# Causal mask by relu, exp and a multiply on GpSimd in place of triangle matmuls on TensorE

## The reference, cut to what matters

```
xn = layernorm(x)                                   # x: 4 x 1024 x 256
q, k, v = xn @ Wq.T + bq, xn @ Wk.T + bk, xn @ Wv.T + bv   # 16 heads of 16
q, k = rope(q), rope(k)
att = where(tril, q @ k.T / 4, -inf)                # causal: key index <= query index
y = softmax(att) @ v                                # merged heads
attn = y @ Wo.T + bo
# feed-forward: 1024 hidden units in 16 blocks of 64; each token keeps its 4 best blocks
mask = top4(softmax(xn @ router_w.T + router_b))
ffn = relu(where(mask, xn @ w1.T + b1, 0)) @ w2.T + b2
out = x + attn + ffn
```

## Time and profile before

| | us |
|---|---|
| median of 3 runs (854.21 to 854.64) | 854.6 |
| profiled execution, time | 853.66 |
| profiled execution, span | 851.9 |
| PE busy | 816.7 |
| DVE busy | 591.8 |
| ACT busy | 426.9 |
| POOL busy | 281.6 |

### The profile page before, as it was taken

The page is one execution under the profiler, slowest core; times in us unless marked ns, Lnnn a source line. Parts: engine busy times, 40 slices in busy tenths (PEclk is TensorE's granted clock), DMA queues, the critical chain, the costliest instruction groups (busy, mean ns, idle before and its releaser), DMA issues.

```text
span 851.9 us, 14875 instructions
## 1 busy us (share of the span) xinstructions
PE 816.7 (96%) x5278; PEld 494.4 (58%) x5278; DVE 591.8 (69%) x1800; ACT 426.9 (50%) x1018; POOL 281.6 (33%) x298
## 2 busy tenths in 40 slices
PE   5784999999999999999999999999999999999998
PEld 4463745554546555664766565565666656465664
DVE  7993887868799856667687766767566876668312
ACT  2410355556565554645564464555456554456462
POOL 3155451926344029406515007706250103000000
PEclk9987999999999999999999999999999999999999
DMA  7445331523251445131251414324242224200021
GB/s 261 165 147 153 106 89 52 163 88 100 77 181 34 113 137 164 57 109 36 77 172 42 105 40 135 110 76 101 75 115 100 49 72 142 54 3 26 3 69 50
DMA packets 52375, 81.91 MB, mean 96 GB/s; under 512 B 5836, under 2 KB 21132, under 8 KB 52300
## 3 DMA queue, kind: packets, MB, share of 16 engines
q1 hardware_dynamic: 52300, 80.95, 31.8%
HBM read 43.06 MB, written 37.88 MB: 95 GB/s over the span
## 4 chain that ended last, share of the span: by engine, by line
PE 85%; DVE 4%; ACT 3%; issue 3%; SPq 2%; DMA 2%; POOL 1%; ACTq 0%; DVEq 0%; POOLq 0%
PE o_bank L1118 15%; PE banks L1043 14%; PE banks L1102 14%; PE banks L1031 12%; PE banks L1018 12%; PE banks L992 5%; PE banks L1105 3%; PE banks L1070 3%; ACT probs L919 3%; PE banks L1001 3%; PE banks L1022 2%; DVE o_norm L1410 1%; DMA bv_sb<-in_bv 1%; DMA term_scratch<-pieces 1%; SPq L604 1%
## 5 line engine op out<-in xcount | busy, mean ns | idle before, releaser
L919 ACT ACTIVATE probs<-banks 128x512 f32<-128x512 f32 (+3 forms) x768 | 328.3, 497 | 247.9 <-PE banks L1105 174.3
L1102 PE MATMUL banks<-q_st,k_st 99*128 99x512 bf16 (+3 forms) x768 | 237.1, 328 | 3.4 <-ACT probs L919 0.8
L1043 PE MATMUL banks<-k_st,q_st 96*128 96x512 bf16 (+3 forms) x768 | 229.0, 328 | 1.5 <-issue 0.8
L1314 DVE CUSTOM_DVE_ANT_0 banks<-banks,tri,part_max 128x512 f32<-128x512 f32 (+3 forms) x256 | 129.7, 554 | 72.6 <-PE banks L1043 41.8
L1311 DVE TENSOR_REDUCE part_max<-banks 128x1 f32<-128x512 f32 x256 | 159.6, 680 | 16.3 <-PE banks L1043 15.7
L1314 DVE CUSTOM_DVE_ANT_0 banks<-banks,tri 128x512 f32<-128x512 f32 (+3 forms) x256 | 120.2, 516 | 30.6 <-PE banks L1043 29.1
L1018 PE MATMUL banks<-xnT,w_sb 128*128 128x256 f32 x512 | 137.6, 392 | 0.7 <-ACT probs L919 0.4
L797 POOL TENSOR_SCALAR max_neg<-row_max 128x16 f32<-128x16 f32 x32 | 8.1, 253 | 384.2 <-DVE row_max L1314 384.2
L1118 PE MATMUL o_bank<-probs,v_sb 128*17 128x512 f32 (+3 forms) x1536 | 133.2, 487 | 0.0
L1031 PE MATMUL banks<-w_sb,hT 128*128 128x256 f32 x512 | 121.2, 383 | 0.2 <-DVE row_max L1314 0.2
L1043 PEld LDWEIGHTS banks<-k_st,q_st 96*128 96x128 bf16 x768 | 73.5, 98 | 72.7 <-issue 21.4
(11 more groups left out here) (97 smaller groups left out, 748.4 us busy)
## 6 DMA issues: line engine op xcount, KB each, us to landing
term_scratch<-pieces SPq DMA_DIRECT2D x84, 256.0 KB
q_st<-term_scratch SPq DMA_DIRECT2D x16, 768.0 KB, 6.9
k_st<-term_scratch SPq DMA_DIRECT2D x16, 768.0 KB, 9.0
y_scratch<-o_norm SPq DMA_DIRECT2D x31, 256.0 KB, 2.5
acc<-in_x SPq DMA_DIRECT2D x8, 512.0 KB, 4.4
rope_sb<-y_scratch SPq DMA_DIRECT2D x15, 256.0 KB
out<-acc SPq DMA_DIRECT2D x7, 512.0 KB, 3.0
x_sb<-in_x SPq DMA_DIRECT2D x3, 1024.0 KB, 7.2
```

Source lines behind the costliest of these rows:

```text
L919: nc.scalar.activation(probs[:, h, PROBS_AT[u]:PROBS_AT[u] + w], filled("score", n, k, h)[:, 0:w], ACT.Exp, scale=SCALE).then_inc(s_out, 1)
L1043: nc.tensor.matmul(bank[:, 0:w], q_st[0:KROWS, at, h, i * P:(i + 1) * P], k_st[0:KROWS, at, h, c * HALF:c * HALF + w], start=True, stop=Tr ...
L1102: last = nc.tensor.matmul(bank[:, 0:w], k_st[0:SROWS, at, h, j * P:(j + 1) * P], q_st[0:SROWS, at, h, q0:q0 + w], start=True, stop=not dia ...
L1314: ins = nc.vector.tensor_tensor_reduce(bank[:, 0:w], bank[:, 0:w], tri[:, HALF - w:HALF], 1.0, least, ALU.add, ALU.max, to)
```

## The change

The triangle matmul goes. For a diagonal unit ScalarE now writes relu(-s) of the square to `probs` (s is the score less its maximum, so it is at most 0 where the mask lets it through, and the relu keeps masked entries finite), the exponential of the rest of the unit as before, and after the fourth head one exponential with scale -SCALE over the four squares together. GpSimd then multiplies the four squares by `keep`, a square of zeros and ones, and `pv` of that unit waits for it (`masked`).

GpSimd is now in the planner (`pump`, `POOL`): its works are put in order with their costs, masks first, then splits of maxima, then the steps of the rotation, the normalisation of x and the biases one by one. A maxT goes when the planner has its split, and a pv run also waits for its masks. Beside that: the copy of bv over 128 columns moves from VectorE to GpSimd; the layer norm factors of batch 1 move from ahead of the first maxima on VectorE into group 0 (`NORMALISED`); the placing of the first maxima goes ahead of the stores of the third projection's pieces on SP; and the scratch tensor of the pieces is laid out heads, d, terms, tokens, so that a store writes its 64 or 128 rows as one dimension and not as heads x 16.

```diff
-NORMALISED = {3: 2, 7: 3}
+NORMALISED = {0: 1, 3: 2, 7: 3}
+SPLIT, PLACE = 1200, 16000
+POOL = {"mask": 3000, "split": 3600, "sin": 5640, "cos": 5640, "add": 5640, "high": 2500, ...
...
     def do_run():
+        while diagonal(*UNITS[(stop - 1) % NU]) and masked.get(stop - 1, clock + 1) > clock:
+            clock += 50
+            pump()
...
             def store_other_pieces(r):
-                    sp.dma_start(term_scratch[0, r, GH:2 * GH, t], pieces[GH * HD:P, r, piece, :]).then_inc(
+                    sp.dma_start(term_rows(0, r, t)[GH * HD:P], pieces[GH * HD:P, r, piece, :]).then_inc(
...
             load_stacks(1)
+            place_maxima(0, 0)
             store_pieces(0, 2)
-            place_maxima(0, 0)
-            store_pieces(0, 3)
...
+            pool.wait_ge(bias_in, 16 * 5)
+            nc.gpsimd.tensor_copy(bv_wide, bv_sb[:, :, None].broadcast_to([P, KB, P])).then_inc(bv_spread, 1)
...
+            def mask(u):
+                if MASKED[u] == 1:
+                    pool.wait_ge(keep_in, 16)
+                pool.wait_ge(exped, EXPED[u])
+                square = probs[:, :, PROBS_AT[u]:PROBS_AT[u] + P]
+                nc.gpsimd.tensor_tensor(square, square, keep[:, None, :].broadcast_to([P, GH, P]),
+                                        ALU.mult).then_inc(masked, 1)
...
-                nc.scalar.activation(probs[:, h, PROBS_AT[u]:PROBS_AT[u] + w], filled("score", n, k, h)[:, 0:w],
-                                     ACT.Exp, scale=SCALE).then_inc(s_out, 1)
+                at, bank = PROBS_AT[u], filled("score", n, k, h)
+                if not diagonal(c, j):
+                    nc.scalar.activation(probs[:, h, at:at + w], bank[:, 0:w], ACT.Exp, scale=SCALE).then_inc(s_out, 1)
+                    return
+                diag = probs[:, h, at:at + P]
+                if w == P:
+                    nc.scalar.activation(diag, bank[:, 0:P], ACT.Relu, scale=-1.0).then_inc(s_out, 1)
+                else:
+                    nc.scalar.activation(diag, bank[:, 0:P], ACT.Relu, scale=-1.0).then_inc(clamped, 1)
+                    nc.scalar.activation(probs[:, h, at + P:at + w], bank[:, P:w], ACT.Exp, scale=SCALE).then_inc(s_out, 1)
+                if h == GH - 1:
+                    if w == P:
+                        act.wait_ge(s_out, S_COUNT["score", n, k, h])
+                    else:
+                        act.wait_ge(clamped, CLAMPED[u])
+                    diag = probs[:, :, at:at + P]
+                    nc.scalar.activation(diag, diag, ACT.Exp, scale=-SCALE).then_inc(exped, 1)
...
-                if diagonal(c, j):
-                    last = nc.tensor.matmul(bank[:, 0:P], tri_k, identb[:], start=False, stop=True)
...
                 pe.wait_ge(s_out, S_COUNT["score", n, k, GH - 1])
+                if diagonal(c, j):
+                    pe.wait_ge(masked, MASKED[u])
...
             dve.wait_ge(rope_in, 32)
-            dve.wait_ge(bias_in, 16 * 5)
-            nc.vector.tensor_copy(bv_wide, bv_sb[:, :, None].broadcast_to([P, KB, P])).then_inc(bv_spread, 1)
...
             turn_halves(0, 3)
-            ln_stats(1, *range(NT))
-            ln_factors(0, NT)
```

More of the change, by code:

```diff
@@ L210 @@
 LATE, FREED = 460, 370
-NORMALISED = {3: 2, 7: 3}
+SPLIT, PLACE = 1200, 16000
+POOL = {"mask": 3000, "split": 3600, "sin": 5640, "cos": 5640, "add": 5640, "high": 2500, "rest": 5100, "mid": 2500,
+        "low": 5100, "xn": 1580, "bias": 5700}
+CHAIN = ("sin", "cos", "add", "high", "rest", "mid", "low")
+RELOAD = 60000
+NORMALISED = {0: 1, 3: 2, 7: 3}
 def arrange():
@@ L225, in arrange, with pool_work, pump @@
     scored, maxed, summed, exps, begun = 0, 0, 0, {}, False
-    placed, to_turn, turned, chores = {}, turned_maxima(), [], []
+    placed, chores = {}, []
+    to_turn = [(n, half) for n in range(GROUPS) for half in range(2)]
     wide, values_free = True, 0
+    pool, pool_todo, pool_free, split, masked = [], [], 0, {}, {}
+    def pool_work(ready, *works):
+        pool_todo.extend((ready, what) for what in works)
+    def pump():
+        nonlocal pool_free
+        while pool_todo and pool_free <= clock:
+            able = [todo for todo in pool_todo if todo[0] <= clock]
+            if not able:
+                return
+            todo = min(able, key=lambda todo: ("mask", "split").index(todo[1][0]) if todo[1][0] in ("mask", "split") else 2)
+            pool_todo.remove(todo)
+            pool.append(todo[1])
+            pool_free = max(pool_free, todo[0]) + POOL[todo[1][0]]
+            if todo[1][0] == "mask":
+                masked[todo[1][1]] = pool_free
+            elif todo[1][0] == "split":
+                split[todo[1][1:]] = pool_free + SPLIT
     def engine_of(kind):
@@ L264, in do_score @@
         order.append(what)
[L265 removed]
+        wide = width(k) > P
         scored += 1
[L267 removed]
+        read(what, fill(what, width(k)), 11 * width(k) // 5 + (30 if not diagonal(*UNITS[k]) else 80 if width(k) == P else 180))
+        if h == GH - 1 and diagonal(*UNITS[k]):
+            ready["scalar"] += 1150
         exps[scored] = free[bank[what]]
+        if h == GH - 1 and diagonal(*UNITS[k]):
+            pool_work(exps[scored], ("mask", n * NU + k))
     def run_end():
@@ L278, in do_norm, with probs_ready @@
         do_chore()
+    def probs_ready(stop):
+        u = stop - 1
+        return masked.get(u, clock + 1) <= clock if diagonal(*UNITS[u % NU]) else exps[stop * GH] <= clock
     def do_run():
@@ L333, in do_chore @@
         ready["vector"] += CHORE[what[0]]
+        if what[0] == "turn":
+            pool_work(ready["vector"], *((step,) + what[1:] for step in CHAIN))
+        elif what[0] == "newton" and not any(chore[2] == what for chore in chores):
+            pool_work(ready["vector"], *(("xn", what[1], t) for t in range(NT)))
     def turn_ready():
-        count, n, half = to_turn[0] if to_turn else (0, GROUPS, 0)
-        return n < GROUPS and (maxed >= count or maxed == len(maxima) and scored >= (GROUPS - 1) * NU * GH + 6)
+        return bool(to_turn) and split.get(to_turn[0], clock + 1) <= clock
     def do_turn():
         work = to_turn.pop(0)
-        do_work([("maxT",) + work[1:]])
-        turned.append(work[1:])
+        do_work([("maxT",) + work])
+        placed[work] = ready["vector"] + PLACE
     def max_ready():
```

172 lines of the change are left out of this document (89 added, 83 removed).

## The result

The changed kernel takes 840.74 us (840.43 to 840.97, 4 runs) against 854.62 us of the kernel before (854.21 to 854.7, 4 runs), a ratio of 0.9838 [0.9821, 0.9855]: 13.9 us faster. The prediction was 825.3 us, 29.3 us faster. The direction held, less than half of the size came. The time lies outside the forecast's own 812 to 837 us and inside the whole range only because that takes in the rivals.

The account below looks back on a forecast made before the run. PE, busy 96% of the span, was taken as the bound: 853.66 - 29.2 (triangles) - 19 (start) + 16 (stretch) + 2.9 (end) = 824.4 us, median 0.9 above, 825.3; own range 812 to 837, 8-in-10 range 806 to 845.

Parts of the forecast that it names:

- The triangles: Diagonal units: removing 512 triangle matmuls of 0.057 us gives back 29.2 us, all on PE's path, their weight loads hidden.
- The start: Before the first score: four edits remove PE's waits and slow clock, gain 19 us, bounds 10 to 22.
- Part (a): Start, VectorE: without bv's 8.00 us copy ahead of the first rotation, the chain to the first stack moves up some 6 us.
- Part (b): Start, stores of pieces: laid out as rows they use more DMA engines; 2 to 3 us at the old rate, counted as hidden.
- Part (c): Start, VectorE: batch 1's layer norm no longer delays the first maximum, begun at 58.82 though ready at 56.36; no price.
- Part (d): Start, GpSimd and SP: first split and write of maxima no longer wait behind stores, so PE's 10.80 us wait goes.
- ScalarE, GpSimd and the end: Costs: 7 us for ScalarE in diagonal quartets, 6 and 3 for late masks, maxima and banks, 2.9 at the last quartet.
- Rival 1: Start: GpSimd's memset blocks the first rotation's multiplies until 25.10, as it did the copy; 8 us more, 833; chance 0.12.
- Rival 2: Behind the first score: the stretch gives the triangles back, 1 us lost per quartet, 32 instead of 16 us: 841; chance 0.15.
- Rival 3: Diagonal quartets: GpSimd's masks at or beyond 2.355 us are the bound; slower than before, 873 at 2 us per quartet; chance 0.05.
- Rival 4: Start: the edits do nothing since another chain is as late; 19 becomes 8, time 836; chance 0.05.
- The sign of being wrong that names PE's waits for ScalarE: PE's queue waiting for masked or for ScalarE by more than 30 us in sum would show the forecast wrong.

Follow-up runs that it names:

- e4: The changed kernel in its own order with one exp per head on diagonal units and without GpSimd's multiplies, so no mask: 822.15 us.
- e13: The kernel before with the start edits, but batch 1's layer norm statistics and factors on VectorE ahead of its first maximum, as before: 842.85 us.
- e9: The kernel before with the start edits, but the copy of bv back on VectorE ahead of the first rotation: 840.98 us.
- e10: The kernel before with the start edits, but the scratch tensor of the pieces laid out heads, terms, d, tokens as before: 839.73 us.
- e5: The kernel before with its triangles, plain exponentials and planner, and the edits of the start alone: 833.25 us.

## Why the prediction was wrong

- **The triangles: the step that failed.** The prediction put "512 x 0.057 = 29.2 us. All of it is on PE's path". The count and the 0.057 were right, the path was not: 16.1 us in the new order, 15.3 in the old. PE "busy" 99.64 of 100 us was taken for a full PE, though the prediction itself says that the records overlap. The waits for banks stand on the weight loads, which it called hidden and did not read. In the kernel before, PEld's waits from 94 us on would have told; among the first lines are

```profile
PEld banks L1102 <- ACT probs L919: 21.4, 64, 0.7
...
PEld o_bank L1118 <- ACT probs L919: 11.0, 37, 0.4
```

What the runs showed in its place: in the diagonal quartets TensorE already ran partly at the pace at which ScalarE and VectorE hand back banks, so that 13.1 of the 29.2 us turned into waits. In the old order, where 13.9 were missing, 4.5 come from the length of the two readers' work and about 1 from a transfer of maxima; the cause of the other 8 stays open. The 13.1 us are most of the 15.4 by which the forecast was off.
- **The order: not in the sum.** The prediction priced what the planner adds, not what its new order does to the rest: 5.0 us. The start gave 2.4 us more than forecast and the new work cost 0.3 less, so that 13.1 + 5.0 - 2.4 - 0.3 = 15.4.
- **The start.** Forecast 19, measured 21.4; first score forecast at 75.3, measured 72.14. But the parts were priced wrongly. Part (a), bv's copy, at about 6 plus clock, is 7.7. Part (b), the layout, was "hidden" and is 6.5. Part (c), the layer norm, had no price and is 9.6. Part (d), GpSimd's and SP's order, carried the 10.8 us of PE's wait and, beside the other three, is 0: that wait had several causes in a row, and taking the earlier ones away took it too. The row that tells this is that of GpSimd's first cast of a piece, which in the kernel before waited for stores until 72.32 us (SP issued the load behind the same stores at 72.23):

```profile
72.32 1.04 POOL L772 CAST pieces<-rope_sb 128x1024 bf16<-128x1024 f32 x1 [15.17 <-issue]
```

- **ScalarE, GpSimd and the end.** Forecast 7 + 9 + 2.9 = 18.9 us, measured 18.6 together. The sum is right by luck, since its parts are not: ScalarE has 12.7 to 15.2 of it, where 7 was forecast for the stretch, and the masks 3.4 to 5.9, where 9 was. "I count 7 us" came from laying ScalarE's length beside PE's as if a third of the quartets were hit; with banks already short nearly all are: against e4, 27 of the 32 quartets are longer in the changed kernel, by 0.07 to 1.5 us. ScalarE's lengths were somewhat overrated too: 2.06 / 4 counts the tail of the last record, and the starts lie 0.48 us apart at 512 columns, not 0.515. ACT is busy 508.0 us, where "near 570" was forecast. At the end, the last pv run ends 10.7 us behind the quartet's first score, forecast 10.9. Before it was 9.2 (839.48 + 2.35 - 832.67), which the prediction read as 8.9. In e4 it is 8.4, so that the new work costs 2.3 us there, forecast 2.9.

```profile
824.54 1.73 PE L1187 MATMUL o_bank<-probs,v_sb 128*17 128x512 f32 x16
827.29 0.62 PE L1187 MATMUL o_bank<-probs,v_sb 128*17 128x256 f32 x8 [1.03 <-POOL probs L851]
828.63 0.41 PE L1187 MATMUL o_bank<-probs,v_sb 128*17 128x128 f32 x8 [0.72 <-POOL probs L851]
```

- **The rivals.** Rival 1 (the memset blocks the first multiplies) is out: in the changed kernel they took 0.69 us each under the memset (14.90 to 25.23). So the trace agrees with the rule that the prediction took from the Trainium skill (SBUF — State Buffer, "Who interferes with whom"). Rival 2 had the right time, 841, by luck. It had the new work cost 32 us in the stretch; less the 2.3 of the end that work cost 16.3, near the forecast's 16. What was missing came from triangles that had never been wholly on the path, and from the order. Rival 3: masks took 1.27 us and GpSimd stayed at 53%. Rival 4: the start did all that was forecast, and more. The sign of being wrong that names PE's waits for ScalarE (over 30 us in sum) could not decide: with the weight loads counted they were 48.4 us already before, and for PE alone 8.0 after.

## What to carry to other kernels

Before a removed instruction is priced at its full length, look at the start-to-start steps of the instructions around it: where they are longer than their columns, a reader sets the pace, and only part of the length comes back, here 16.1 of 29.2 us. Read the waits of the weight loads beside those of the matmuls. A wait seen in a trace may have several causes in a row; undo one edit at a time to learn which pays, and don't add a wait's length for the last of them. When a change bundles a start, an order and a mask, run the parts by themselves: here the start alone (833.25 us) beats the whole (840.74 us).

## What the runs showed of the hardware

- A short VectorE instruction with SBUF inputs (8 elements) takes 0.17 us between or behind GpSimd's tensor operations of 2.35 us and up to 2.27 us beside one (e13); the copy with one SBUF input took 8.00 and 8.84 us beside GpSimd's memset (before and e9), while multiplies with two inputs ran under the same memset in 0.69 us.
- ScalarE's records overlap as PE's do. In the changed kernel's last quartet relus of 128 columns hold it for 0.16 us and exponentials of 384 for 0.37, whatever the records' own lengths. In the kernel before, exponentials in a row start 0.48 us apart at 512 columns, 0.37 at 384, 0.26 at 256 and 0.16 at 128. Of the changed kernel:

```profile
818.81 0.28 ACT L982 ACTIVATE probs<-banks 128x128 f32<-128x128 f32 x1 [3.07 <-PE banks L1172]
818.98 0.48 ACT L983 ACTIVATE probs<-banks 128x384 f32<-128x384 f32 x1
819.35 0.28 ACT L982 ACTIVATE probs<-banks 128x128 f32<-128x128 f32 x1
819.51 0.51 ACT L983 ACTIVATE probs<-banks 128x384 f32<-128x384 f32 x1
```

- The layout of the scratch tensor changed the rate of the stores. From the first of the twelve stores to the load that waits for them SP took 20.6 us with the old layout (e10, 45.66 to 66.27) and 11.3 with the new one (e5, 38.19 to 49.48). In the changed kernel the twelve stores start at 39.4 us, beside a load of 768 KB; from 30 to 50 us, in 40 slices, the GB/s are as follows, where before they were a flat 102:

```profile
GB/s 111 45 213 25 119 143 0 29 213 205 201 201 197 209 213 201 176 107 98 352 324 242 213 246 193 152 197 188 332 274 340 369 397 406 397 385 365 344 266 94
```
